# Second attention of a four-layer model: two heads weighed together in two column quarters of TensorE, and VectorE's counts and maxima reordered around a branch

## The reference, cut to what matters

```python
scores = einsum('bhqd,bhkd->bhqk', q, k) / sqrt(8)
attn = softmax(scores, axis=-1)
k_keep = maximum(1, (L * (1.0 - sr)).astype(int32))    # sr: one number per head
rank = argsort(argsort(-attn, axis=-1), axis=-1)
w = where(rank < k_keep[None, :, None, None], attn, 0.0)
w = w / (sum(w, axis=-1, keepdims=True) + 1e-10)
out = einsum('bhqk,bhkd->bhqd', w, v)                  # then out @ Wo.T + bo
```

## Time and profile before

| what | value |
|---|---|
| median of 3 runs | 2046.71 us (2041.70 to 2064.53) |
| the profiled execution | 2043.58 us, span 2041.8 us |
| mean granted TensorE clock over the span | 0.791 |
| second attention's loop, first to last settling instruction | 585.19 to 1069.17 us |
| time between settling instructions, iterations 0 to 6 | 72.25, 70.76, 71.05, 70.76, 69.46, 70.06, 59.65 us |
| instructions of L1758 (weighing) in all | 1024 matmul records, 205.4 us of TensorE's busy time |

### The profile page before, as it was taken

One profiled execution on the slowest core, in us unless ns is written; L12 is line 12 of the kernel. 1 busy time (PEld: TensorE's weight loads), 2 busy tenths in 40 slices (PEclk: granted clock), 3 DMA queues, 4 the chain that ended last, 5 costly groups with the idle time before them and its releaser, 6 DMA issues.

```text
span 2041.8 us, 38862 instructions
## 1 busy us (share of the span) xinstructions
PE 1642.0 (80%) x12640; PEld 1172.7 (57%) x12640; DVE 1476.3 (72%) x4747; ACT 1115.7 (55%) x3322; POOL 877.4 (43%) x1162
## 2 busy tenths in 40 slices
PE   3888989897358988988779978527777799999978
PEld 3445667675236766766668645413443477777763
DVE  6678776555588988999887842358876777887657
ACT  2444444445988898899852423214452366666620
POOL 3333221124253554444433577676300377767610
PEclk8889999997555555555557989858896899999969
DMA  4111101003000000000001023322110000000000
GB/s 139 47 47 41 40 21 42 18 2 122 15 9 17 12 13 11 17 9 9 1 1 59 23 78 110 97 65 73 48 72 20 15 1 1 2 1 2 1 1 21
DMA packets 67305, 67.58 MB, mean 33 GB/s; under 512 B 9955, under 2 KB 58966, under 8 KB 66566
## 3 DMA queue, kind: packets, MB, share of 16 engines
q1 hardware_dynamic: 58930, 53.09, 7.9%
q0 software_dynamic: 5120, 10.50, 2.0%
q10 hardware_dynamic: 3040, 1.38, 0.2%
HBM read 30.41 MB, written 8.39 MB: 19 GB/s over the span
## 4 chain that ended last, share of the span: by engine, by line
PE 35%; DVE 27%; ACT 12%; issue 10%; POOL 6%; SPq 6%; ACTq 2%; DMA 1%; DVEq 0%; POOLq 0%
SPq L689 5%; POOL weights L1165 4%; DVE weights L3212 3%; PE bank L2143 3%; PE bank L1551 3%; PE bank L2103 3%; ACT big L4445 3%; PE bank L1567 3%; DVE weights L3156 3%; DVE nmax L3072 2%; DVE small L3200 2%; PE bank L1758 2%; PE bank L2130 2%; ACT rope_s L4235 2%; ACT rope_c L4235 2%
## 5 line engine op out<-in xcount | busy, mean ns | idle before, releaser
L1758 PEld LDWEIGHTS bank<-V,probsT 128*128 128x128 f32 x1024 | 203.6, 297 | 28.4 <-ACT probsT L4246 13.7
L1758 PE MATMUL bank<-V,probsT 128*128 128x9 f32 x1024 | 205.4, 333 | 15.2 <-ACT probsT L4246 10.9
L2711 DVE TENSOR_REDUCE nmax<-bank 128x4 f32<-128x1024 f32 x144 | 175.9, 1221 | 51.8 <-PE bank L1331 48.8
L891 POOL TENSOR_TENSOR big<-big,rinv 128x512 f32<-128x512 f32 x128 | 131.7, 1049 | 45.7 <-DVE rinv L3767 45.7
L1745 PE MATMUL bank<-silu_b,weights 128*128 128x128 bf16 x464 | 138.9, 303 | 0.0
L4050 ACT ACTIVATE feat_o<-bank 128x1024 f32<-128x1024 f32 x72 | 73.7, 1023 | 101.5 <-PE bank L1331 66.7
L4050 ACT ACTIVATE O<-bank 128x1024 f32<-128x1024 f32 x72 | 73.7, 1024 | 97.2 <-PE bank L1331 70.6
L3761 DVE TENSOR_REDUCE nmax<-bank 128x2 f32<-128x512 f32 x128 | 81.9, 682 | 58.1 <-PE bank L2103 58.1
L4445 ACT ACTIVATE big<-bank,nmax 128x256 f32<-128x256 f32 x256 | 117.6, 478 | 11.1 <-DVE nmax L3761 11.1
L4453 ACT ACTIVATE big<-bank 128x512 f32<-128x512 f32 x128 | 73.8, 614 | 68.8 <-PE bank L2130 68.8
L4246 ACT ACTIVATE probsT<-bank 128x512 f32<-128x512 f32 x128 | 75.9, 600 | 58.4 <-PE bank L1745 39.0
(11 more groups left out here) (818 smaller groups left out, 5110.5 us busy)
## 6 DMA issues: line engine op xcount, KB each, us to landing
qT<-parts SPq DMA_DIRECT2D x276, 32.0 KB
big<-V SPq DMA_DIRECT2D x192, 32.0 KB
y_rows<-weights SPq DMA_DIRECT2D x24, 256.0 KB, 2.3
big<-parts SPq DMA_DIRECT2D x180, 32.0 KB
weights<-in_weights_l_ffn SPq DMA_DIRECT2D x1, 4832.0 KB, 14.3
weights<-in_weights_l_attn SPq DMA_DIRECT2D x1, 3904.0 KB, 13.0
qT<-V SPq DMA_DIRECT2D x96, 32.0 KB
weights<-in_weights_l_ffn SPq DMA_DIRECT2D x1, 2860.0 KB, 11.7
```

The source lines that it names most:

```text
L891: nc.gpsimd.tensor_tensor(row, row, rinv[:, h % H, :].unsqueeze(2).to_broadcast([P, T, S]), ALU.mult).then_inc(scaled.sem, 1)
L1758: last = mm(pb[1][:, t * S + h * wide:t * S + (h + 1) * wide], probsT[:, h % 2, at:at + P], values_of(b, k)[:, h * wide:(h + 1) * wide], s ...
L2711: V_.tensor_reduce(to, scored.rearrange("p (i a n) -> p i a n", i=HPG, n=n), AX.X, ALU.max, negate=True).then_inc(score_max.sem, 1)
```

## The change

`l1_weigh` of one head becomes `l1_weigh_two` of heads 2u and 2u+1. The values (9 columns of a head) are now the stationary operand and stand in a quarter of the array's columns given by h % 4; the turned probabilities of both query tiles (256 columns) move. The sums of four heads come out transposed, in four strips of partitions of bank 1's first half. ScalarE's new `l1_take_quad` copies these 128x256 to SBUF, and TensorE's new `l1_turn_quad` multiplies each half of that with 36 columns of the identity, which turns them back to tokens in rows, into the second half of bank 1 (the last four heads into the first half). `weighed` waits for four such quads and works in two pieces. In TensorE's list pair u stands where head 2u+1 was weighed, and the places of the even heads fall away; quads 0, 1 and 2 get places of their own, and quad 3 stands behind the next iteration's doubts. In VectorE's list `count_below` of round 1 moves from behind `l1_max(n + 2, 0)` to the front of the iteration, and `ask_doubt` ahead of the two `largest_of`, which then stand between it and the register load. Two signals of another phase (`z_psum`, `z_ready`) are renamed and shared; that part of the diff is left out.

```diff
@@ -57,6 +57,7 @@
+QUADS = H // 4
@@ -473,6 +474,10 @@
         values_of = lambda b, t: V[:, t, ones_at(b)]
         minus_two = silu_b[:, 0:P // 2].bitcast(BF16)
+        weighed_quad = V[:, 0, 576:576 + S]
+        early_heads = 3 * H // 4
+        weighed_at = ((slice(0, early_heads), pb[1][:, S:S + T * early_heads * (HD + 1)]),
+                      (slice(early_heads, H), pb[1][:, 0:T * (H - early_heads) * (HD + 1)]))
         first_rows = front_n[:].rearrange("p t d -> p (t d)")
         tried_first = [first_rows[:, 64 * i:64 * (i + 1)].rearrange("p (u j) -> p u j", u=2) for i in range(2)]
@@ -605,8 +610,8 @@
         ranks_psum = wide_signal("ranks_psum", l1_ffn=3, l2_ffn=2 * PAIRS)
 
-        z_psum = signal("z_psum", l2_ffn=1)
-        z_ready = signal("z_ready", l2_ffn=1)
+        side_psum = signal("side_psum", l1_attn=QUADS, l2_ffn=1)
+        side_taken = signal("side_taken", l1_attn=QUADS, l2_ffn=1)
 
         rope_ready = signal("rope_ready", l3_attn=2 * NQ3)
@@ -1745,19 +1750,30 @@
                 last.then_inc(probsT_psum.sem, 1)
 
-            def l1_weigh(b, h, ph="l1_attn"):
-                if h == 0:
+            def l1_weigh_two(b, u, ph="l1_attn"):
+                if u == 0:
                     pe.wait_ge(qkv_ready.sem, qkv_ready(ph, b, 2))
                     if b:
                         pe.wait_ge(tok_ready.sem, tok_ready(ph, b - 1, 1))
-                pe.wait_ge(probsT_ready.sem, probsT_ready(ph, b, h + 1))
+                pe.wait_ge(probsT_ready.sem, probsT_ready(ph, b, 2 * u + 2))
                 wide = HD + 1
-                for t in range(T):
-                    for k in range(T):
-                        at = t * S + k * P
-                        last = mm(pb[1][:, t * S + h * wide:t * S + (h + 1) * wide], probsT[:, h % 2, at:at + P],
-                                  values_of(b, k)[:, h * wide:(h + 1) * wide], start=k == 0, stop=k == T - 1)
-                last.then_inc(pv_done.sem, 1)
+                for k in range(T):
+                    for h in (2 * u, 2 * u + 1):
+                        part = slice(32 * (h % 4), 32 * (h % 4) + wide)
+                        by_keys = probsT[:, h % 2, :].rearrange("p (t k n) -> p k t n", t=T, k=T)
+                        last = mm(pb[1][part, 0:S].rearrange("p (t n) -> p t n", t=T), values_of(b, k)[:, h * wide:(h + 1) * wide], by_keys[:, k],
+                                  start=k == 0, stop=k == T - 1)
+                last.then_inc(pv_done.sem, 2)
+
+            def l1_turn_quad(b, q, ph="l1_attn"):
+                pe.wait_ge(side_taken.sem, side_taken(ph, b, q + 1))
+                of_heads = C("ident").rearrange("p (j d) -> p j d", j=4)[:, :, 0:HD + 1]
+                heads_there, there = weighed_at[q // 3]
+                at = 4 * q - heads_there.start
+                for t in range(T):
+                    o = there.rearrange("p (t h d) -> p t h d", t=T, d=HD + 1)[:, t, at:at + 4, :]
+                    last = mm(o, weighed_quad[:, t * P:(t + 1) * P], of_heads, start=True, stop=True)
+                last.then_inc(side_psum.sem, 1)
 
             def l1_doubt(b, ph="l1_attn"):
@@ -1792,6 +1808,8 @@
                     if now(n):
                         l1_doubt(n)
+                    if now(n - 1):
+                        l1_turn_quad(n - 1, QUADS - 1)
                     if now(n + 2):
                         l1_values(n + 2)
@@ -1805,12 +1823,10 @@
                     if now(n + 3):
                         l1_project(n + 3)
-                    if now(n):
-                        l1_weigh(n, 0)
                     if now(n - 1):
                         l1_turn_out(n - 1)
                     if now(n):
-                        l1_weigh(n, 1)
+                        l1_weigh_two(n, 0)
                         l1_turn_probs(n, 2)
                     if now(n + 2):
@@ -1820,51 +1836,48 @@
                     if now(n):
                         l1_turn_probs(n, 3)
-                        l1_weigh(n, 2)
                         l1_turn_probs(n, 4)
                     if now(n + 3):
                         l1_turn_keys(n + 3)
                     if now(n):
-                        l1_weigh(n, 3)
+                        l1_weigh_two(n, 1)
                         l1_turn_probs(n, 5)
                         l1_turn_probs(n, 6)
...
                         l1_scores(n + 2, 5)
                     if now(n):
-                        l1_weigh(n, 4)
+                        l1_turn_quad(n, 0)
                     if now(n + 2):
                         l1_scores(n + 2, 6)
                     if now(n):
                         l1_turn_probs(n, 7)
-                        l1_weigh(n, 5)
+                        l1_weigh_two(n, 2)
                     if now(n + 3):
                         l1_gram(n + 3)
...
                         l1_scores(n + 2, 7)
                     if now(n):
-                        l1_weigh(n, 6)
                         l1_turn_probs(n, 8)
                     if now(n + 2):
...
                         l1_spread(n + 3)
                     if now(n):
-                        l1_weigh(n, 7)
+                        l1_weigh_two(n, 3)
                         l1_turn_probs(n, 9)
                         l1_turn_probs(n, 10)
-                        l1_weigh(n, 8)
+                        l1_turn_quad(n, 1)
                     if now(n + 2):
                         l1_scores(n + 2, 9)
...
                     if now(n):
                         l1_turn_probs(n, 11)
-                        l1_weigh(n, 9)
+                        l1_weigh_two(n, 4)
                     if now(n + 2):
                         l1_scores(n + 2, 11)
...
                     if now(n):
                         l1_turn_probs(n, 12)
-                        l1_weigh(n, 10)
                     if now(n + 2):
                         l1_scores(n + 2, 13)
@@ -1874,13 +1887,13 @@
                     if now(n):
                         l1_turn_probs(n, 13)
-                        l1_weigh(n, 11)
-                        l1_weigh(n, 12)
+                        l1_weigh_two(n, 5)
                         l1_turn_probs(n, 14)
+                        l1_turn_quad(n, 2)
                         l1_turn_probs(n, 15)
-                        l1_weigh(n, 13)
-                        l1_weigh(n, 14)
-                        l1_weigh(n, 15)
+                        l1_weigh_two(n, 6)
+                        l1_weigh_two(n, 7)
+                l1_turn_quad(B - 1, QUADS - 1)
                 l1_turn_out(B - 1)
                 l1_project_out(B - 1)
@@ -3213,18 +3226,25 @@
 
             def weighed(b, ph="l1_attn"):
-                dve.wait_ge(pv_done.sem, pv_done(ph, b, H))
+                dve.wait_ge(side_psum.sem, side_psum(ph, b, QUADS))
                 if b:
                     dve.wait_ge(turned.sem, turned(ph, b - 1, 1))
-                wide = H * (HD + 1)
-                o1 = tiles(pb[1])[:, :, 0:wide].rearrange("p t (h d) -> p t h d", h=H)
                 sums_by_tile = sums_of(b).rearrange("p h t -> p t h")
-                link(V_.scalar_tensor_tensor(kept_sum, sums_by_tile, 1e-10, o1[:, :, :, HD], ALU.mult, ALU.add))
+                for of, there in weighed_at:
+                    o1 = there.rearrange("p (t h d) -> p t h d", t=T, d=HD + 1)
+                    link(V_.scalar_tensor_tensor(kept_sum[:, :, of], sums_by_tile[:, :, of], 1e-10, o1[:, :, :, HD], ALU.mult, ALU.add))
                 linkup()
                 link(V_.reciprocal(kept_sum, kept_sum))
                 linkup()
-                V_.tensor_tensor(tokens1.rearrange("p t (h d) -> p t h d", h=H), o1[:, :, :, 0:HD],
-                                 kept_sum.unsqueeze(3).to_broadcast([P, T, H, HD]), ALU.mult).then_inc(tok_ready.sem, 1)
+                for of, there in weighed_at:
+                    o1 = there.rearrange("p (t h d) -> p t h d", t=T, d=HD + 1)
+                    heads_there = of.stop - of.start
+                    last = V_.tensor_tensor(tokens1.rearrange("p t (h d) -> p t h d", h=H)[:, :, of], o1[:, :, :, 0:HD],
+                                            kept_sum[:, :, of].unsqueeze(3).to_broadcast([P, T, heads_there, HD]), ALU.mult)
+                    if of.stop == H:
+                        last.then_inc(tok_ready.sem, 1)
+                    else:
+                        link(last)
 
             def l1_result(b, ph="l1_attn"):
@@ -3265,17 +3285,18 @@
                 l1_gates()
                 for n in range(-1, B):
+                    if now(n + 1):
+                        count_below(n + 1, 0)
                     if now(n):
+                        ask_doubt(n)
                         largest_of(n, 0)
                         largest_of(n, 1)
-                        ask_doubt(n)
                         settle_doubt(n)
                         all_but_past(n, 0)
...
                         l1_max(n + 2, 0)
                     if now(n + 1):
-                        count_below(n + 1, 0)
```

(20 more changed lines are left out.)

## The result

The changed kernel takes **2095.47 us** (median of 4 runs, 2088.63 to 2098.06) against 2049.80 (2041.7 to 2064.53) for the kernel before in the same comparison: a ratio of 1.0215, 95% interval 1.0179 to 1.0252. It is slower by about 46 us; the forecast was 2080, slower, within 2036 to 2108. Its profiled execution took 2098.06 us, with a span of 2096.3 and a granted clock of 0.807 over the whole span. The medians of the experiments leave out four executions that took 7 to 99% longer than the others of their kernel (one each of runs 2, 4 and 10 and of the kernel before).

A forecast was written before the change was run, and what follows sets the result against it. VectorE's own work plus some 5 us at the branch was taken to bound an iteration. Six iterations losing 6 us (36), iteration 6 winning about 2 and iteration 7 losing 1 gave +35 on 2043.58: 2079, forecast 2080, range 2036 to 2108.

The forecast's parts named there:

- Held takes: ScalarE's takes 8, 10, 12 and 14 come late, since a pair empties both `probsT` slots only when it ends.
- a late sum: The doubts' sum, behind the last pair on TensorE, comes at 76.0 us behind settling against 66.9, at the lower level.
- a covered branch: Eight MAX8 on VectorE cover 2.7 us of the branch; idle time at settling falls to 1 to 1.5 us.
- The schedule of the lower level: An iteration's steps at TensorE's lower clock, 1.9 us a pair: settling at 80.5, 9.5 us more an iteration.
- I take 6: Loss in us per iteration of the second attention, taken between 9.5 (lower clock level) and 0.4 (upper).
- the row at 770.34: Profile row of the kernel before: the old weighing took 1.05 us there, the upper clock level, against 1.82 at 788.92.
- the sum of 2079: Six iterations at 6 us, 36; iteration 6 wins about 2, iteration 7 loses 1: +35 on 2043.58.
- the likeliest case: The stalls of held takes weigh as summed: 2060 to 2095 us, chance 0.55.
- the 1 us forecast for iteration 7: Last iteration: a quad's copy, turning and division in a row cost about 1.5 us, quicker pairs give back 0.5.
- The clock rises: Rival: moving columns lift TensorE's clock through the stage, every step at the upper level: 2045 us, no change; chance 0.20.
- Stalls in full or more: Rival: clock stays low (+9.5 an iteration), or the branch stays uncovered, or pairs do not overlap: 2090 to 2125; chance 0.15.
- Faster: Rival: ScalarE absorbs the held takes, the doubts' sum is not late, VectorE wins 3.0 us an iteration: 2024; chance 0.10.

The follow-up runs named there:

- run 2: The changed kernel with VectorE's order of before (pairs, quads and new matmul form stay): 2094.55 us, ratio 1.0228.
- run 4: The changed kernel, but each head weighed by itself at its old place with its own release, third quad's copy ahead of take 13: 2043.38 us, ratio 0.9980.
- run 10: The changed kernel with a third slot and quad 2's copy ahead of take 13, but VectorE's order of before: 2039.37 us, ratio 0.9943.
- run 1: The kernel before with VectorE's reorder alone (old matmul form, one head at a time, no quads): 2056.13 us, ratio 1.0033.
- run 3: The kernel before with VectorE's reorder, two heads weighed in the old form at the pair's place, slots given back together: 2133.27 us, ratio 1.0412.
- run 5: The changed kernel with a third slot for turned probabilities, so even takes no longer wait for the pair just before: 2050.92 us, ratio 1.0004.
- run 7: The changed kernel with two slots, only quad 2's copy moved ahead of take 13: 2068.15 us, ratio 1.0076.
- run 8: The changed kernel with two slots, only pair 4 moved ahead of scores 9, 10 and turn 11: 2080.34 us, ratio 1.0146.
- run 6: The changed kernel with a third slot and quad 2's copy moved ahead of take 13: 2034.87 us, ratio 0.9916.
- run 9: The changed kernel with two slots, every pair moved right behind what its second take unlocks, third quad's copy ahead of take 13: 2050.12 us, ratio 1.0014.

## Why the prediction came out as it did

**The mechanism was right.** Held takes, a late sum and a covered branch are what the trace shows, and runs 1 to 5 show that the coupling is their cause. The schedule of the lower level, in us behind the settling instruction of iteration 2 (746.59), stands beside the rows above:

| step | forecast, lower level | measured |
|---|---|---|
| take 8 | 38.7 | 39.3 |
| take 10 | 49.6 | 50.2 |
| take 12 | 60.1 | 60.2 |
| quad 2's copy | 68.1 | 67.7 |
| take 14 | 72.4 | 72.4 |
| copy of the doubts' sum | 76.0 | 76.0 |
| next settling | 80.5 | 80.2 |

**The term that was mis-sized is "I take 6".** Measured are 8.1 us an iteration (48.4 / 6), near the lower level's end. I had gone down to 6 because TensorE would work some ten us without a gap, from turning 12 to turning 14, and "behind such a run the row at 770.34 shows the upper level". In the trace of after this stretch of iteration 2 stays at the lower level from its start to its end (the granted clock is the third number from the right):

```profile
799.82:809.05 9.23, 8.38 (x43) 4.51 (x42) 9.12 (x37) 4.96 (x20) 5.26 (x9) 0.50 0.07 21
```

Pairs 4, 5 and 6 of this iteration take 1.88 each, and only pair 0, where nothing is held, takes 1.04; over iterations 0 to 4, pairs 4 to 6 take 1.58 to 1.88. So iterations 0 to 4 lost 7.3 to 9.6 us, and iteration 5, which has less of the following batches' work, 5.7. At 48.4 instead of 36, the sum of 2079 becomes 2091, 4 us from the median. The median itself lies 0.5 us above the likeliest case's 2060 to 2095.

**Prices.** A pair at the lower level takes 1.88 (forecast 1.9), at the upper 1.04 (1.1); quad's turning 1.06 (1.03), its copy 0.37 (0.38). From the copy of the sum to settling 4.16 us (4.5 forecast, 4.15 before): the branch's idle time fell from 3.87 to 1.14, within the forecast 1 to 1.5, and the MAX8 fill the rest. The remark that eight records one after the other would take "over twice" 1.08 was too high: four of a single head take 1.03 (last section), from which I estimate some 1.9 for eight; the overlap stands without it. In iteration 6 the gain is 1.8 (59.65 to 57.84; forecast 2).

**The rest.** Up to the first settling instruction the profiled execution of after is 3.1 us later than that of before, and behind the last one 4.8 longer. Runs 7 and 8, which have the same instructions up to there, reach the first settling at 583.4 and 582.0 (after: 588.3), so the 3.1 belongs to differences between executions. From the last settling to the end run 7 needs 977.2, as after does (977.4), and run 8 971.1; so how much of the 4.8 is the 1 us forecast for iteration 7 stays open.

**The rivals.** *The clock rises* was half right. It did rise, from 0.54 to 0.63 over the six iterations, and the time rose with it: in iteration 2 pair 0's row is at the upper level, those of pairs 4 to 6, behind held takes, at the lower, and these set the time. The Trainium skill, "TensorE: Matmul & The Clock Gate", Part 1, has the clock follow how busy the engine has been. The means of whole windows are not in that order: 370 of 424 us busy at 0.54, 308 of 473 at 0.63, and 308 of 427 at 0.78 in run 4, where the pace is that of before. That does not refute the page, since the same records are also busy longer at a lower clock (34.25 and 44.32 us in run 1). *Stalls in full or more* came nearest by its price (9.5 an iteration against 8.1, and the median lies within its 2090 to 2125), but the branch is covered and the pairs overlap, which its other two reasons denied. *Faster* needed the sum by 66.2; it came at 76.0. Run 6 shows what that rival was worth with nothing held: 69.5 us an iteration (417.0 / 6), 1.2 below the 70.7 of before, not 3, since VectorE then waits for ScalarE's counts (run 10).

## What to carry to other kernels

When two steps are joined, look first at when the buffers they read are given back: here one release for two heads, behind everything that TensorE's order put ahead of the second head, turned a step of half the price into a loss of 2%. Either the joined step goes right behind the last thing it needs, or its buffers get one slot more; the first makes what stood ahead of it later, and others may wait for that (run 9); with a third slot and one copy moved, the same pairs were 0.8% faster than the kernel before. And price a wait at the clock level of the stretch where it is held, not at the mean of the stage.

## What the runs showed of the hardware

Two heads side by side in two column quarters cost no more than one. In run 4 a head by itself has four records (pairs have eight, at 1.88 and 1.04):

```profile
755.88 1.88 PE L1763 MATMUL bank<-probsT,V 128*9 128x256 f32 x4
...
762.59 1.03 PE L1763 MATMUL bank<-probsT,V 128*9 128x256 f32 x4
```

The Trainium skill, "TensorE: Matmul & The Clock Gate", Part 3, has matmuls of different column tiles run at once; the trace agrees, for f32 and without any loss: 1.88 for one head or two.

And a stretch with the same 263 matmul records took 37.8 us at a granted 0.73 and 47.9 at 0.57 (run 1): 10.1 us, where six iterations won 2.2 by the reorder.
